# Six score banks where no maxima are made, and the last unit's row sums by VectorE and over its last steps

## What is computed

```python
def xattn(x, context, mask, Wq, Wk, Wv, Wo, bo, g1, b1, g2, b2):
    xn, cn = layer_norm(x, g1, b1), layer_norm(context, g2, b2)
    q, k, v = heads(xn @ Wq.T), heads(cn @ Wk.T), heads(cn @ Wv.T)
    scores = where(mask, q @ k.T / sqrt(32), -inf)
    return merge(softmax(scores) @ v) @ Wo.T + bo
x = x + xattn(layernorm(x), ctx, ...)
x = x + layernorm_then_fp6_quantise(x) @ quantised(weight).T + bias
```

## Time and profile before

| | |
|---|---|
| runs | 4574.81, 4576.45, 4580.00 us, median 4576.45 |
| profiled execution | 4573.34 us, of which the span of the trace is 4571.5 us |
| PE busy | 4377.7 us, 96% |
| DVE busy | 3408.7 us, 75% |
| POOL busy | 2984.5 us, 65% |
| ACT busy | 2834.4 us, 62% |
| granted TensorE clock | 0.997 of full speed |

### The profile page before, as it was taken

The page is one execution under the profiler, slowest core; times in us unless marked ns, Lnnn a source line. Parts: engine busy times, 40 slices in busy tenths (PEclk is TensorE's granted clock), DMA queues, the critical chain, the costliest instruction groups (busy, mean ns, idle before and its releaser), DMA issues.

```text
span 4571.5 us, 89848 instructions
## 1 busy us (share of the span) xinstructions
PE 4377.7 (96%) x37008; PEld 1505.2 (33%) x37008; DVE 3408.7 (75%) x3879; ACT 2834.4 (62%) x5128; POOL 2984.5 (65%) x1818
## 2 busy tenths in 40 slices
PE   5999999999999999999999999999999999999998
PEld 2322243222432234322342223422234222342223
DVE  5788467885688846888568885688856888668875
ACT  3478744786447864487545875458754578446784
POOL 2288853887438874388744887348873588726886
PEclk9999999999999999999999999999999999999999
DMA  5255632557325563356633565335554365543653
GB/s 193 68 121 117 153 127 63 121 115 179 101 66 120 121 171 101 67 120 121 167 99 74 115 124 162 103 77 121 113 161 108 78 122 112 155 112 77 124 115 95
DMA packets 190014, 532.38 MB, mean 116 GB/s; under 512 B 28625, under 2 KB 102673, under 8 KB 148386
## 3 DMA queue, kind: packets, MB, share of 16 engines
q0 software_dynamic: 43776, 318.79, 34.7%
q1 hardware_dynamic: 145826, 207.83, 14.8%
HBM read 110.98 MB, written 21.01 MB: 29 GB/s over the span
## 4 chain that ended last, share of the span: by engine, by line
PE 75%; DVE 11%; ACT 6%; POOL 4%; issue 3%; DMA 1%; SPq 0%; DVEq 0%; ACTq 0%; POOLq 0%
PE banks L978 20%; PE banks L990 19%; PE banks L892 15%; PE banks L952 11%; PE banks L1016 6%; ACT region L771 5%; DVE max_parts L606 4%; PE banks L861 2%; PE banks L886 2%; POOL wkT_wvT_wqT L418 1%; DVE x_stats L521 1%; DVE region L695 1%; DVE amax L554 1%; DVE qscale L556 1%; ACT values L846 1%
## 5 line engine op out<-in xcount | busy, mean ns | idle before, releaser
L606 DVE TENSOR_REDUCE max_parts<-banks 128x2 f32<-128x1024 f32 x2048 | 2402.2, 1219 | 448.4 <-PE banks L952 436.8
L771 ACT ACTIVATE region<-banks 128x512 f32<-128x512 f32 x4096 | 2210.9, 597 | 541.3 <-PE banks L978 440.1
L418 POOL TENSOR_TENSOR wkT_wvT_wqT<-region 128x1024 f32<-128x1024 f32 x608 | 1491.4, 2562 | 660.2 <-ACT region L771 655.3
L978 PE MATMUL banks<-queries_stacked,keys_stacked 98*32 98x512 f16 x16384 | 1356.7, 384 | 68.3 <-ACT region L771 48.7
L990 PE MATMUL banks<-region,values 128*32 128x512 f32 x8192 | 1074.4, 598 | 17.9 <-ACT region L771 7.7
L978 PEld LDWEIGHTS banks<-queries_stacked,keys_stacked 98*32 98x32 f16 x16384 | 412.0, 94 | 1277.7 <-ACT region L771 997.6
L952 PE MATMUL banks<-keys_stacked,queries_stacked 33*128 33x512 f16 x4096 | 699.2, 385 | 6.6 <-DVE max_parts L606 3.5
L892 PE MATMUL banks<-region,wkT_wvT_wqT 128*128 128x512 f16 x2304 | 558.1, 381 | 13.2 <-DMA wkT_wvT_wqT<-weights_split 10.4
L418 POOL TENSOR_TENSOR sums<-region 128x1024 f32<-128x1024 f32 x160 | 399.6, 2610 | 127.4 <-ACT region L771 127.0
L400 POOL TENSOR_TENSOR region<-row_sums_inverse,region 128x512 f16<-128x512 f32 x80 | 93.4, 1168 | 431.1 <-ACT region L746 430.7
L892 PE MATMUL banks<-wkT_wvT_wqT,region 128*128 128x512 f16 x1536 | 368.8, 380 | 0.0
(11 more groups left out here) (88 smaller groups left out, 3225.2 us busy)
## 6 DMA issues: line engine op xcount, KB each, us to landing
wdT<-wkT_wvT_wqT POOLq DMA_DIRECT2D x96, 1024.0 KB, 11.8
wkT_wvT_wqT<-wkT_wvT_wqT POOLq DMA_DIRECT2D x80, 1024.0 KB, 7.2
sums<-wkT_wvT_wqT POOLq DMA_DIRECT2D x72, 1024.0 KB, 7.3
wkT_wvT_wqT<-sums POOLq DMA_DIRECT2D x40, 1024.0 KB, 7.0
region<-in_x SPq DMA_DIRECT2D x24, 1024.0 KB, 7.6
wkT_wvT_wqT<-weights_split SPq DMA_DIRECT2D x8, 3072.0 KB, 16.6
keys_stacked<-region SPq DMA_DIRECT2D x384, 64.0 KB, 2.0
keys_stacked<-sums SPq DMA_DIRECT2D x384, 64.0 KB, 2.0
```

Of the source, the lines that this page charges most:

```text
L418: e.tensor_tensor(SUMS[dst][:, half], PR[i][:, half], PR[i + 1][:, half], ALU.add).then_inc(s_pr, 1)
L606: e.tensor_reduce(mpart[:, buf, :, a, t, c], MXB[parity], AX.X, ALU.max).then_inc(s_mxd, 1)
L771: e.activation(PR[u % 4][:, j * HALF:j * HALF + HALF], score_bank(kt, j)[0], ACT.Exp, scale=SCALE).then_inc(s_ex, 1)
L978: mm = e.matmul(dst[HD * t:HD * t + HD, :], KA[0:STR, ds(ka + (j * C + (u + 1) * P + HD * t), HD)], QA[0:STR, ds(qa[j], HALF)], start=True ...
```

## The change

It has four parts.

1. `wide(n, tile)` is true for all tiles of unit 7 and for tiles 9 to 15 of unit 6. There the scores rotate over six banks (4, 5, 0, 1, 2, 3), the first ones waiting until VectorE has reduced the last maxima, and `step` makes all four scores of the next tile ahead of the weighted values (`ahead`). Tile 8 of unit 6 goes back to two banks. Bank 7 is left alone in unit 6's late tiles, so unit 7's turned maxima go there (`turn_bank`), behind the copy of the row sums.
2. In the last unit GpSimd adds nothing. It issues `merge_last` and the three merges and goes on to the residual.
3. VectorE does the adds (`last_sums`): pairs 0 to 3 as before, pair 4 into `second`, and the four tiles of pairs 5 and 6 are added to `second` one after the other. It begins with the multiplication of unit 5's output, which stood in unit 6, and has unit 6's inversion and multiplication between pairs 3 and 4.
4. In the last unit the clearing of LB and the contraction of `PR[2]` move from step 15 to step 14, and step 15 contracts three sources instead of six: `PR[3]`, `second`, `first`.

```diff
+        turn_bank = lambda n: PS[0:J * QT, 7 if n == NU - 1 else 4, 0:P]
+        def wide(n, tile):
+            return n == NU - 1 or n == NU - 2 and tile >= 9
+
-        def score_bank(tile, j):
-            if tile < 8:
+        def score_bank(n, tile, j):
+            if wide(n, tile):
+                slot = 4 * (KT * (n - NU + 2) + tile - 9) + j
+                return bank((4, 5, 0, 1, 2, 3)[slot % 6]), 2 if slot < 2 else 6 if slot >= 6 else None
+            if tile < 8 or n == NU - 2:
                 return bank(4 + j % 2), 2
...
@@ gpsimd
+                        if end:
+                            merge_last()
+                            merge(0, 1, one)
+                            merge(1, 2, two)
+                            merge(2, 3, three)
+                            continue
...
@@ vector
+                    def last_sums(m):
+                        first, one, two, three, second = buffers(n)
+                        late = b * (2 * NU - 2) + 2 * n
+                        def made(t, h):
+                            e.wait_ge(s_ex, m * (KT * J) + t * J + 2 * h + 4)
+                        def pair(p, dst):
+                            i = 2 * (p % 2)
+                            for h in range(2):
+                                half = ds(2 * HALF * h, 2 * HALF)
+                                made(2 * p + 1, h)
+                                e.tensor_tensor(SUMS[dst][:, half], PR[i][:, half], PR[i + 1][:, half],
+                                                ALU.add).then_inc(s_pr, 1)
+                        def add(t, last_of_pair):
+                            for h in range(2):
+                                half = ds(2 * HALF * h, 2 * HALF)
+                                made(t, h)
+                                ins = e.tensor_tensor(SUMS[second][:, half], SUMS[second][:, half], PR[t % 4][:, half],
+                                                      ALU.add)
+                                if last_of_pair:
+                                    ins.then_inc(s_pr, 1)
+                                else:
+                                    ch.did(ins)
+                        e.wait_ge(s_pr, m * 14 + 2)
+                        normalise(m - 2, n - 2)
+                        e.wait_ge(s_acc, 3 * m * 16)
+                        pair(0, first)
+                        e.wait_ge(s_ac2, (late - 1) * 16)
+                        pair(1, one)
+                        e.wait_ge(s_pv, m * KT + 4 + 3)
+                        pair(2, two)
+                        e.wait_ge(s_ac2, late * 16)
+                        pair(3, three)
+                        invert_first(m - 1)
+                        invert_rest()
+                        normalise(m - 1, n - 1)
+                        e.wait_ge(s_pv, m * KT + 4 + 6)
+                        pair(4, second)
+                        for p in (5, 6):
+                            e.wait_ge(s_pr, m * 14 + 2 + 2 * p)
+                            add(2 * p, False)
+                            ch.settle()
+                            add(2 * p + 1, True)
...
-                    if last:
+                    if last and q == 0:
                         invert_first(m - 1)
                         invert_rest()
-                        normalise(m - 1, n - 1)
...
                     if end:
+                        last_sums(m)
                         invert_first(m)
...
@@ tensor
-                            dst, back = score_bank(tile, j)
-                            e.wait_ge(s_ex, ex + (u + 1) * J + j + 3 - back)
-                            if tile == 8 and j == 0:
-                                e.wait_ge(s_on, m + 1)
-                            if tile == 11 and j == 0 and turning:
-                                e.wait_ge(s_mc, m + 2)
+                            dst, back = score_bank(n, tile, j)
+                            if back:
+                                e.wait_ge(s_ex, ex + (u + 1) * J + j + 3 - back)
+                            elif tile == 9:
+                                e.wait_ge(s_mxd, (b + 1) * NH + 1)
+                            else:
+                                e.wait_ge(s_mxd, (b + 1) * NH + 2)
...
+                    ahead = wide(n, tile) and not (n == NU - 2 and tile == 9)
                     score(0)
                     score(1)
+                    if ahead:
+                        score(2)
+                        score(3)
...
-                    score(2)
-                    score(3)
+                    if not ahead:
+                        score(2)
+                        score(3)
...
                     def turn_next(ex):
-                        e.wait_ge(s_ex, ex + (2 * J + 2))
+                        if last:
+                            e.wait_ge(s_on, m + 1)
+                        else:
+                            e.wait_ge(s_ex, ex + (2 * J + 2))
...
                     for u in range(3):
-                        step(m, ex, ka, qa, v, u, 4 * K3 + u + 1, rows[u])
+                        step(m, n, ex, ka, qa, v, u, 4 * K3 + u + 1, rows[u],
+                             sums=[] if not end or u < 2 else
+                             [(PR[2], None)],
+                             fresh=(s_on, m + 1) if end and u == 2 else None)
...
-                        left = [(PR[3], None), (second, (s_pr, m * 14 + 12)), (one, (s_pr, m * 14 + 14)),
-                                (two, (s_pr, m * 14 + 16)), (first, (s_acc, 48 * (m + 1)))]
+                        left = [(PR[3], None), (second, (s_pr, m * 14 + 16)), (first, (s_acc, 48 * (m + 1)))]
```

More of the change, by code:

```diff
@@ L470, in _ @@
                         merge(2, 3, three)
-                        if not end:
-                            merge_late(5, one)
+                        merge_late(5, one)
                         pair(6, two)
@@ L828, in _ @@
                         turned_maxima(0, 0)
-                exps(b * NU, 0, 0, 0)
+                exps(b * NU, 0, 0)
                 for g in range(0, G - 1):
@@ L958, in turn_maxima, with step @@
                     e.wait_ge(s_nm, m + 1)
-                    e.matmul(TURN, nmax[:, buf, :], ident[:, :], start=True, stop=True).then_inc(s_mt, 1)
-                def step(m, ex, ka, qa, v, u, tile, row=None, after=None, sums=(), end=False, between=None, scores=True,
-                         weigh=True, fresh=None, closing=False, turning=True):
+                    e.matmul(turn_bank(m % NU), nmax[:, buf, :], ident[:, :], start=True, stop=True).then_inc(s_mt, 1)
+                def step(m, n, ex, ka, qa, v, u, tile, row=None, after=None, sums=(), end=False, between=None, scores=True,
+                         weigh=True, fresh=None, closing=False):
                     if row:
@@ L1025, in unit @@
                 def unit(g, q, last):
-                    m = (b * NU + 2 * g + q)
+                    n = 2 * g + q
+                    m = b * NU + n
                     end = last and q == 1
@@ L1056, in quad @@
                                     sums = [(SUMS[4], (s_ac2, 16 * (b * (2 * NU - 2) + 2 * (2 * g + q))))]
-                            step(m, ex, ka, qa, v, u, t + 1, rows[u], sums=sums, closing=t == 5,
-                                 between=(lambda: turn_next(ex)) if t == 9 and not end else None, turning=not end)
+                            step(m, n, ex, ka, qa, v, u, t + 1, rows[u], sums=sums, closing=t == 5,
+                                 between=(lambda: turn_next(ex)) if t == 9 and not end else None)
                     clear(OB, s_oc, m + 1)
@@ L1064, in unit @@
                     ex, ka, v, rows = at(K3, J - 1, g + 1, q, not last)
+                    first, one, two, three, second = (SUMS[i] for i in buffers(n))
                     for u in range(3):
[L1067 to L1069 removed]
+                        step(m, n, ex, ka, qa, v, u, 4 * K3 + u + 1, rows[u],
+                             sums=[] if not end or u < 2 else
+                             [(PR[2], None)],
+                             fresh=(s_on, m + 1) if end and u == 2 else None)
                     if end:
[L1071 to L1073 removed]
+                        left = [(PR[3], None), (second, (s_pr, m * 14 + 16)), (first, (s_acc, 48 * (m + 1)))]
+                    else:
+                        left = [(PR[2], None)]
                     nqa = None if end else [((2 * ng + nq) * (J * HALF) + j * HALF) for j in range(J)]
[L1075 to L1077 removed]
+                    step(m, n + 1, ex, ng * (J * C) - 4 * P, nqa, v, 3, 0, rows[3],
+                         None if end else (s_mr, 64 * (m + 2)), left, True, scores=not end, closing=end,
+                         fresh=None if end else (s_ex, ex + (4 * J + 2)))
                 front()
@@ L1083, in _ @@
                 e.wait_ge(s_vv, b * KT + KT)
-                step(b * NU, b * (NU * KT * J) - J, -P, [j * HALF for j in range(J)], 0, 0, 0, weigh=False)
+                step(b * NU, 0, b * (NU * KT * J) - J, -P, [j * HALF for j in range(J)], 0, 0, 0, weigh=False)
```

23 lines of the change are left out of this document (11 added, 12 removed).

## The result

The changed kernel takes 4504.5 us in the median (4502.4 to 4507.7), the kernel before 4577.4 on the same chip: 0.984 of it, with an interval of 0.9828 to 0.9852. The forecast was 4501 us, with 4478 to 4540 as its range.

The account below looks back on a forecast made before the run. TensorE and ScalarE wait for each other in turn, GpSimd's adds limit second, then the unit's end. 8.0 + 2.6 - 1.2 = 9.4 us a batch, 75 for eight: 4498, plus 3.1 for the median, 4501 us; range 4478 to 4540.

Parts of the forecast that it names:

- Start of unit 7: Unit 6 into unit 7: output copy moves ahead of the wait for GpSimd's last pair, tile 1 starts 2.1 us earlier.
- Pace: Unit 7, tiles 1 to 15: exponentials 0.49 us apart without waits for scores, 60 in 29.5 us; VectorE's adds 1.2 us each.
- step 14's sum: Unit 7, step 14: the added row sum has no score behind it and is hidden within tile 15's 1.97 us.
- The two early sums: Unit 7, sums of steps 0 and 2: they make a later score late, costing 0.35 us each.
- Step 5's wait: Unit 7, step 5: the sum waits for the late merge by DMA, delaying tile 7's scores 1.9 us; bounds 0.35 and 4.7.
- Last exponential: End of unit 7's exponentials: at 548.3 instead of 556.27, 8.0 us earlier, the 2.1 at the start included.
- Tail: After the last exponential: 24 of 48 row-sum matmuls go, saving 2.6 us, less 1.2 us for the collision.
- the collision: Unit end: VectorE's last multiply meets GpSimd's two bias adds, charged 1.2 us a batch; bounds 0 and 1.5.
- the step stays above ScalarE's pace: Rival, chance 0.17: unit 7's steps take 2.25 us, gain 5.2 us a batch, 4535 us.
- Slower: Rival, chance 0.05: in unit 7 VectorE's add is as slow as GpSimd's, 2.65 us; +8.9 us a batch, 4648 us.
- Late DMA and collision cost little: Rival, chance 0.18: step 5's merge and the multiply's meeting with bias adds cost little; 11 to 12.1 us gained, 4479 to 4488.
- Nothing moves: Rival, chance 0.05: the late DMA comes so late, about 7 us later than said, that it eats the gain.

Follow-up runs that it names:

- adds_three_banks: Changed kernel with only VectorE's adds and the short last step; late scores rotate over three banks in the old order: 4555.3 us, 0.9947 of the kernel before.
- no_late_dma: Changed kernel without the late merge of unit 6's last pair; TensorE contracts that buffer in step 1 of unit 7: 4482.9 us, run again (`no_late_dma_again`) 4485.2.
- double_pairs: Changed kernel with each of VectorE's ten pair adds of the last unit made twice: 4528.2 us, 0.9888 of the kernel before.
- project_first_early: no_late_dma with first projection before the last sums, inversion and multiply behind the first residual add, earlier last add and next-token load: 4490.6 us, 0.9805.
- one_merge: no_late_dma with one DMA merge left in the last unit; TensorE contracts first, two and three in steps 8, 10 and 12: 4493.2 us, 0.9812.

## Why the prediction was right

The working was made for batch 0, so the terms can be laid beside all eight. Times run from the start of line 435's DMA (444 in the changed kernel) in unit 6.

*Start of unit 7: 2.1 us expected.* Tile 1 came 517.72 - 508.73 = 8.99 us after that DMA, and now 516.19 - 509.29 = 6.90: 2.1 us. Right, and GpSimd's last pair is the releaser, as said.

*Pace: right.* 0.49 us an exponential, VectorE's add 1.19 us (1.2), step 14's sum hidden. The two early sums were a little too cheap in the working: it charged 0.35 us each, by a latency of 0.2 us that no row gave. ScalarE's idle time is 0.34 and 0.36 us, but in a stream each exponential starts before the one ahead of it ends. Counted from start to start the two steps are 0.98 and 1.03 us instead of 0.49, so they cost about 0.5 us each.

*Step 5's wait: right where the DMAs took their medians, too small in the mean.* Expected were 1.9 us. ScalarE's hole was 4.54 (and 0.88 behind it), 1.90, 0.61, 1.07, 3.82, 3.42, 1.91 and 0.51 us in the eight batches, 2.2 in the mean without the 0.88. Line 444's DMA landed after 12.9 us in batch 0, as I had put it, and after 11.3 to 13.0 in all eight. The term that was mis-sized in batch 0 is the merge behind it (line 442, now 451): it landed 8.5 us after its issue in batches 0 and 5 and 7.7 in batch 4, and 7.0 in the five others, where I took the median of 7.0. In batches 1 and 6, where both DMAs took what I had put down, the hole is 1.9. In batches 2, 3 and 7 line 444's DMA landed 0.9 to 1.6 us early. That the mean is near 1.9 is owed to early and late landings that balance. The holes of seven batches lie in the stated 0.35 to 4.7 us; batch 0 with 4.54 + 0.88 does not. What the sum lacked is the lower clock: it fell at 530.3 us in batch 0 and at 2752.3 in batch 4, before TensorE's waits of 2.91 and 2.19 us were over. In batch 0 that cost 2.0 us, and in batch 4 some 1.1 us: the hole is 1.63 us longer than TensorE's wait there, and 0.55 us in batches 1, 5 and 6.

*Last exponential: 8.0 us expected, 7.3 found in the mean of eight* (4.1 in batch 0, 9.1 in batch 7). The two sums and step 5's wait are the difference.

*Tail: 2.6 - 1.2 = 1.4 us expected, 1.2 found, and that this fits is luck.* From the last exponential to the first residual add it was 10.18 us in every batch before. Now it is 7.9, 8.5, 7.4, 14.0, 8.2, 8.7, 7.4 and 9.4. The shorter last step brings 2.8 us: in `adds_three_banks`, where nothing collides, the tail is 7.36 us in every batch. The multiply was held up by 0.3 to 1.1 us in six batches, and in four of these (2, 3, 6 and 7) the first residual add waited for the projection anyway; in two batches it met nothing, and there the first residual add waited 1.2 us for the bias. So the collision costs some 0.5 us in the mean (batches 0, 1, 4 and 5 over 7.36 us), not the 1.2 I charged. What I left out makes up for it: the third merge lands too late for the last sum in batches 3, 5 and 7, worth 1.1 us in the mean by batches 3 and 7. The timeline of TensorE in batch 3:

```profile
2215.99 1.04 PE L1091 MATMUL banks<-wdT,ones 128*32 128x512 f32 x8
2220.51 1.94 PE L1091 MATMUL banks<-sums,ones 128*32 128x512 f32 x8 [3.48 <-DMA sums<-wkT_wvT_wqT]
2222.37 7.12 PE L950 MATMUL banks<-woT,queries_stacked 128*128 128x512 f32 x11
```

3.48 us of waiting, and then sums and the first projection at half speed (the granted clock is 0.50 from 2219.9 to 2226.7). The merges follow each other (each waits for the landing of the one before), and the first of them, issued while the late merge is in flight, takes 9.8 to 11.7 us to land, where it takes 7.2 to 8.8 in `no_late_dma`. In the prediction I looked at the late merge alone and took the other three as covered, and they were not.

*Sum.* 7.34 + 1.24 = 8.6 us a batch, 69 us from unit 6's end to the first residual add over eight batches. The span fell by 65.6. The other 3 us lie elsewhere, at least in part in the clock: at the start of batch 0's attention it is 0.60 from 207 to 210 us, ahead of anything that the change touches, and that batch enters unit 6 some 0.75 us later than before. Such a stretch is absent from `no_late_dma_again`, so it varies from one execution to the next. The mean granted clock is 0.993, before 0.997. The medians differ by 72.9 us; forecast were 75.

The rivals: "the step stays above ScalarE's pace" fell with the 0.49 us. "Slower" fell with the add's 1.19 us; double_pairs shows it would have come from there. "Late DMA and collision cost little" held in batch 2 alone (11.9 us). "Nothing moves" needed a descriptor port held by VectorE. The issues of the merges that VectorE's adds overlap (522.44, 536.48 and 544.65 in batch 0) took 0.87 to 0.89 us, no longer than the earlier trace rows shows. This agrees with the exception that the Trainium skill (SBUF — State Buffer, "Who interferes with whom") makes, by inference, for tensor_tensor. The multiply and GpSimd's bias adds did hold each other up (1.78 us for a multiply of 0.69, and 1.71 us for a bias add of 1.26), but these were the longest.

## What to carry to other kernels

When two engines feed each other in a ring, look for a third that keeps the same pace: here the new order alone moved the last exponential by 3.0 us, the faster adds alone by 0.6, and both by 7.3. Banks buy nothing by themselves; what counts is that the producer's next work stands ahead of the instruction that waits for the consumer. After a stage is made faster, list every DMA that it waits for with its whole chain of predecessors: a merge that landed 1.9 to 4.2 us before its sum at the old pace is the next limiter, and removing it at the price of 0.86 us of extra matmuls was worth 2.4 us a batch.

## What the runs showed that was not expected

A wait of 2.9 us on TensorE went with 6.8 us at a granted clock of 0.50 in one trace, and in another trace of the same kernel and batch with none; the fall cost 2.0 us. In batch 5 it was the other way round: no fall at 2.87 us of waiting in the first trace, one at 2.61 us in the second. So a wait's price is not only its length, and it varies from run to run. And issuing the residual load earlier did not always bring it earlier. In `project_first_early` it landed 5.5 us after its issue where the third merge had landed by 40 us after the start of `merge_late`'s DMA (batches 1, 2, 4 and 7), and 7.7 to 9.8 us where that merge landed at 42.6 to 43.4; each time it came 2.4 us or more behind the merge. In `one_merge`, without that merge, it landed after 5.5 to 5.9 us in every batch.
